# Attention inside a mixture-of-experts layer: PE's projection matmuls and VectorE's work in another order over the eight steps of a unit, and the squares of the roots on GpSimd

## What is computed

```python
q = x @ Wq.T                      # x is layer-normalised
k, v = context @ Wk.T, context @ Wv.T
q, k = rmsnorm(q), rmsnorm(k)     # t * rsqrt(mean(t*t) + 1e-6), per head
attn = softmax(q @ k.T * 16 ** -0.5)
x = x + attn @ v
x = x + moe(layernorm(x))         # 7 experts, 2 per token, and a shared one
```

## Time and profile before

| | us |
|---|---|
| median of 3 runs | 1032.24 |
| lowest, highest | 1028.94, 1035.53 |
| the profiled execution's own time | 1035.61 |
| its span | 1033.8 |
| PE busy, share of the span | 968.9, 94% |
| VectorE busy | 704.0, 68% |
| ScalarE busy | 515.9, 50% |
| GpSimd busy | 145.5, 14% |

### The profile page before, as it was taken

How to read it: one execution, slowest core, us unless ns; L and a number is a source line. 1 busy time by engine, 2 the same in 40 slices (tenths; PEclk the granted TensorE clock), 3 DMA queues, 4 the chain that set the end, 5 groups by cost and what they waited for, 6 DMA issues and landing times.

```text
span 1033.8 us, 18059 instructions
## 1 busy us (share of the span) xinstructions
PE 968.9 (94%) x6730; PEld 701.5 (68%) x6731; DVE 704.0 (68%) x1463; ACT 515.9 (50%) x649; POOL 145.5 (14%) x167
## 2 busy tenths in 40 slices
PE   4899999989999899987799999999999999999995
PEld 3534443345434453332699999999999998999995
DVE  5778767867687756771678776675766767767553
ACT  4578668856787568875334221332423343424311
POOL 1000000000000000000100000233333332433331
PEclk9999999999999999999699999999999999999998
DMA  9100100001000010210342114354363545554533
GB/s 342 66 1 2 41 1 1 4 18 62 1 2 21 11 52 1 83 41 1 103 165 63 62 62 175 74 174 77 74 173 61 183 71 163 148 128 95 152 60 41
DMA packets 28984, 78.93 MB, mean 76 GB/s; under 512 B 7040, under 2 KB 7040, under 8 KB 24832
## 3 DMA queue, kind: packets, MB, share of 16 engines
q1 hardware_dynamic: 18400, 52.31, 14.1%
q0 software_dynamic: 10528, 25.87, 12.5%
HBM read 57.64 MB, written 20.52 MB: 76 GB/s over the span
## 4 chain that ended last, share of the span: by engine, by line
PE 48%; DVE 2%; issue 1%; DVEq 0%; POOL 0%; ACT 0%; POOLq 0%
PE u_ps L1185 15%; PE z_ps L1185 15%; PE y_ps L1185 15%; PE xt_ps L1198 2%; PE z_ps L1179 1%; DVE w_sb L1387 1%; PE y_ps L1211 0%; DVE u_lo L1548 0%; DVE stats L1403 0%; DVE x_lo L1397 0%; DVEq L1029 0%; DVE y_sb L1576 0%; POOL out L1129 0%; PE xt_ps L1171 0%; ACT u_hi L1319 0%
## 5 line engine op out<-in xcount | busy, mean ns | idle before, releaser
L612 ACT ACTIVATE probs<-scores 128x2048 f32<-128x2048 f32 x128 | 240.3, 1878 | 80.8 <-PE scores L267 78.0
L1185 PE MATMUL u_ps<-x_hi,w_sb 128*128 128x256 f32 x896 | 168.0, 285 | 5.0 <-issue 3.1
L1185 PE MATMUL z_ps<-u_hi,w_sb 128*128 128x256 f32 x896 | 169.1, 286 | 0.2 <-DVE u_lo L1548 0.2
L1319 ACT ACTIVATE u_hi<-u_ps,b_ug 128x256 fp32r<-128x256 f32 x112 | 47.0, 471 | 203.8 <-PE u_ps L1185 195.6
L1185 PEld LDWEIGHTS u_ps<-x_hi,w_sb 128*128 128x128 f32 x896 | 143.2, 194 | 7.8 <-issue 4.6
L1185 PEld LDWEIGHTS z_ps<-u_hi,w_sb 128*128 128x128 f32 x896 | 142.4, 193 | 0.4 <-DVE u_lo L1548 0.4
L1185 PE MATMUL y_ps<-w_sb,g_hi 128*128 128x512 f32 x448 | 138.7, 391 | 0.4 <-DVE g_lo L1566 0.4
L283 PE MATMUL o_ps<-probs,v_sb 128*17 128x512 f32 x1024 | 137.5, 609 | 1.0 <-ACT probs L612 1.0
L1185 PE MATMUL u_ps<-x_lo,w_sb 128*128 128x256 f32 x448 | 127.7, 285 | 0.0
L1185 PE MATMUL z_ps<-u_lo,w_sb 128*128 128x256 f32 x448 | 127.1, 284 | 0.0
L267 PEld LDWEIGHTS scores<-q_st,k_hi 32*128 32x128 f32 x512 | 25.1, 183 | 123.8 <-ACT probs L612 71.1
(11 more groups left out here) (216 smaller groups left out, 1567.5 us busy)
## 6 DMA issues: line engine op xcount, KB each, us to landing
w_raw<-w_all SPq DMA_DIRECT2D x27, 1024.0 KB, 6.9
ctx_raw<-ctx_t SPq DMA_DIRECT2D x4, 1024.0 KB, 6.4
out<-x_sb SPq DMA_DIRECT2D x16, 256.0 KB
xg<-xn_dram POOLq DMA_DIRECT2D x14, 256.0 KB
x_sb<-x SPq DMA_DIRECT2D x1, 3072.0 KB, 18.0
xn_dram<-xn SPq DMA_DIRECT2D x12, 256.0 KB, 2.0
bd<-b_down SPq DMA_DIRECT2D x9, 256.0 KB
x_sb<-x SPq DMA_DIRECT2D x4, 256.0 KB, 3.8
```

What stands on the lines that cost most here:

```text
L612: nc.scalar.activation(probs[:, t % 2], scores[:], ACT.Exp).then_inc(p_ready, 1)
L1185: ins = nc.tensor.matmul(out_ps, stat[a], mov[b], start=(first and a + b == 0), stop=(last and a == 1), skip_group_check=True)
L1319: last = nc.scalar.activation(u_hi[:, c, :], u_ps[:, b, a, :], ACT.Identity, bias=b_ug[:, par, 0, c:c + 1])
```

## The change

Projections come in portions of any number of matmuls, set by two tables (`first, end` in the list of the 12). `k_turns` can also come behind the weighing of step 6 (`after`), in the units where a batch follows and g is at least 1. The squares of the roots move from ScalarE to a multiplication on GpSimd. In VectorE's order the second stack of q moves from step 4 of the unit before to step 0 of its own unit, `finalize` of half 1 from step 2 to step 1, Newton's step for k from 6 to 5, the context splits from steps 2, 3, 4, 4 to 1, 2, 2, 3, one normalisation for the batch behind from 1 to 2, the statistics from 0, 1, 6, 7 to 2, 2, 3, 6. The second block of new tokens is split whole on VectorE in step 6 (`norm_both`), where ScalarE made its high part in step 7. q's squares on ScalarE move from step 7 to step 6.

```diff
+        K_TURNS = {6: (0, 4), 7: (4, 5), 0: (5, 9), 1: (9, 12)}
+        Q_TURNS = {3: (0, 5), 4: (5, 9), 5: (9, 12)}
...
+            def root2_q(u):
+                pool.wait_ge(rq_ready, u + 1)
+                pool.wait_ge(norm_done, 2 * u if u else 1)
+                nc.gpsimd.tensor_tensor(r2[:], r0[:], r0[:], ALU.mult).then_inc(r2q_ready, 1)
+
+            def root2_k(u):
+                pool.wait_ge(rk_ready, u + 1)
+                if u:
+                    pool.wait_ge(norm_done, 2 * u + 1)
+                nc.gpsimd.tensor_tensor(r2[:], r0[:], r0[:], ALU.mult).then_inc(r2k_ready, 1)
...
             def between(u, s):
                 b, g, more, behind = batch_of(u)
                 ahead = u + 2 < UNITS
+                if s in (0, 1) and u + 1 < UNITS:
+                    k_turns(u + 1, *K_TURNS[s])
...
-                elif s <= 5:
+                elif s in Q_TURNS:
                     if ahead:
-                        q_passes(u + 2, s - 3)
+                        q_turns(u + 2, *Q_TURNS[s])
...
-                elif ahead:
-                    k_chunk(u + 2, 1)
+                    if ahead and not (more and g >= 1):
+                        k_turns(u + 2, *K_TURNS[s])
+                elif s == 7 and ahead:
+                    k_turns(u + 2, *K_TURNS[s])
                     sum_q(u + 2)
+
+            def after(u, s):
+                b, g, more, behind = batch_of(u)
+                if s == 6 and more and g >= 1:
+                    k_turns(u + 2, *K_TURNS[s])
...
-            def root2_q(u):
-                act.wait_ge(rq_ready, u + 1)
-                act.wait_ge(norm_done, 2 * u if u else 1)
-                nc.scalar.activation(r2[:], r0[:], ACT.Square).then_inc(r2q_ready, 1)
...
                 if s == 0:
-                    stat1(0)
-                    if behind and g == 1:
-                        stat(tile_of(b - 1, 2), mv2[:, 2, :])
                     if more and g == 2:
                         norm_both(b + 1, 2)
+                    if u:
+                        stack_q(u, 1)
...
+                    if more and g == 2:
+                        context_split(b + 1, 0)
                     if nxt:
                         first_root_q(u + 1)
-                elif s == 2:
-                    if more and g == 2:
-                        context_split(b + 1, 0)
                     if u:
                         finalize(u - 1, 1)
+                elif s == 2:
                     if nxt:
                         sums_k(u + 1)
+                    if behind and g == 2:
+                        norm2(b - 1, 1)
+                    if more and g == 2:
+                        context_split(b + 1, 1)
+                        context_split(b + 1, 2)
...
                     if nxt:
                         first_root_k(u + 1)
-                        stack_q(u + 1, 1)
+                        stack_q(u + 1, 0)
...
-                    if more and g == 2:
-                        context_split(b + 1, 2)
-                        context_split(b + 1, 3)
...
+                    if nxt:
+                        newton_k(u + 1)
                     finalize(u, 0)
...
                     if more and g == 1:
                         norm_low(b + 1, 0)
+                        norm_both(b + 1, 1)
```

More of the change, by code:

```diff
@@ L292, in three, with q_turns @@
                 return ins
-            def q_passes(u, part):
+            TURNS = [(c, a, b) for c in range(DC) for a, b in ((0, 0), (0, 1), (1, 0))]
+            def q_turns(u, first, end):
                 g = u % GROUPS
-                if part == 0:
+                if first == 0:
                     begin("b", B_AT, ("q", u), b_free)
@@ L299, in q_passes @@
                     pe.wait_ge(xt_split, (u // GROUPS + 1) * BT)
-                turns = [(c, a, b) for c in range(DC) for a, b in ((0, 0), (0, 1), (1, 0))]
-                for c, a, b in turns[4 * part:4 * part + 4]:
+                for c, a, b in TURNS[first:end]:
                     last = nc.tensor.matmul(bank_b[:], (wq_hi, wq_lo)[a][:, g, c, :], (xt_hi, xt_lo)[b][:, c, :],
@@ L313, in k_chunk @@
                     pe.wait_ge(ctx_split, (u // GROUPS + 1) * MT)
-                last = three(bank_a[:], (wk_hi[:, g, c, :], wk_lo[:, g, c, :]), (ctx_hi[:, c, :], ctx_lo[:, c, :]),
-                             c == 0, c == DC - 1)
-                if c == DC - 1:
+                for c, a, b in TURNS[first:end]:
+                    last = nc.tensor.matmul(bank_a[:], (wk_hi, wk_lo)[a][:, g, c, :], (ctx_hi, ctx_lo)[b][:, c, :],
+                                            start=(c == 0 and a + b == 0), stop=(c == DC - 1 and a == 1),
+                                            skip_group_check=True)
+                if end == len(TURNS):
                     last.then_inc(a_ready, 1)
@@ L442, in _ @@
             v_all(scores[:, 3, :], 0, 3).then_inc(first_v, 1)
-            for part in range(3):
-                q_passes(1, part)
-            k_chunk(1, 0)
-            k_chunk(1, 1)
+            q_turns(1, 0, 12)
+            k_turns(1, 0, 5)
             sum_q(1)
@@ L849, in step @@
                         norm(b + 1, 0)
+                    stat1(0)
+                    stat1(1)
+                    if behind and g == 1:
+                        stat(tile_of(b - 1, 2), mv2[:, 2, :])
                 elif s == 3:
@@ L904, in step @@
                     if more and g == 1:
+                        norm(b + 1, 2)
+                    if behind and g == 2:
+                        norm2(b - 1, 2)
+                else:
+                    if behind and g == 2:
+                        gates_out(b - 1, 0)
+                    if u + 2 < UNITS:
+                        sums_q(u + 2)
+                    if more and g == 1:
                         norm(b + 1, 3)
+                    if nxt:
+                        stack_k(u + 1, 1)
                     if behind and g == 1:
```

111 lines of the change are left out of this document (38 added, 73 removed).

## The result

| | before | after |
|---|---|---|
| median of 20 runs each, us | 1031.59 | 1028.50 |
| lowest, highest | 1028.87, 1035.63 | 1023.33, 1029.82 |
| ratio after/before, 95% interval | | 0.9966 [0.9957, 0.9976] |
| the profiled execution's own time, its span | 1035.61, 1033.8 | 1028.14, 1026.4 |

The change makes the kernel 3.1 to 3.5 us faster, which is within 1%. The forecast of 1024.6 gave it twice that, and the range 1018.0 to 1031.0 held the result. The two profiled executions differ by 7.5 us, almost exactly the 7.6 of the forecast: the first thing to explain is why the medians differ by less than half of it.

What follows compares the result with a forecast made beforehand. PE was taken to carry the attention loop, with waits for VectorE and the exponential's chain. Gains of 3.8, 2.3, 0.2, 3.7, 10.6 less 0.6, 0.2, 7.0, 1.4, 3.8 gave 7.6 us: 1032.2 to 1024.6, range 1018.0 to 1031.0.

Steps and rivals of the forecast that it cites:

- I take the differences over as they are: Gains counted in one profiled execution of 1035.6 us were subtracted unchanged from the median of 1032.24, 3.4 lower.
- the term of 2.3 us for the squares: Step 2 without ScalarE's square returns to 2.72 us, 0.33 gained in each of seven units: 2.3 us.
- the portions' term: Moving projection matmuls between steps gains 0.27 us in each of 14 units, 3.8 us, less 0.6 in seven.
- GpSimd's squares: Each takes 0.51 to 2.7 us, 1.4 taken; hidden in the loop, costing 0.2 us before it.
- Rival B: GpSimd holds VectorE up 0.5 us in units 1, 2, 6, 10, and the clock falls in all four: 1030.4; chance 0.15.
- New tokens: Steps 6 and 7 of units 1, 5, 9: the 1.2 us wait before the q sums goes, 3.7 us gained.
- I find the bank free before PE asks: In units 1, 5, 9, the earlier VectorE split and k behind the weighing leave PE no wait for the bank.
- Units 6 and 10: VectorE's new order removes three waits in steps 4 and 5 and the fallen clock: 5.3 us each, 10.6 together.
- rival D: Waits in steps 4 and 5 of units 6 and 10 stay; half the 10.6 us remains: 1029.9; chance 0.10.
- The new wait: The stack moved to step 0 delays the k sums in units 1, 2, 6, 10: -7.0 us, bounds 0 and -12.
- The clock: Waits of 2.05 us make it fall in units 6 and 10, 1.9 us each: -3.8; units 1, 2 left out.
- rival A: The clock stays up behind the new waits, so the gain is 11.4 us: 1020.8; chance 0.25.

Runs made afterwards that it cites:

- second profile of before: The kernel before, unchanged, run and profiled again: 1030.82 us, ratio 0.9995; the loop of this profile takes 438.7 us against 442.4 in the first.
- e_squares: The kernel before with only the squares of the k and q roots moved from ScalarE to GpSimd: 1032.48 us, ratio 1.0025.
- e_kpool: The kernel before with only k's root squares moved to GpSimd, q's staying on ScalarE: 1032.65 us, ratio 1.0008.
- e_tokens: The kernel before with the new portions, the second new-token block split on VectorE in step 6, and k behind the weighing in units 1, 5, 9: 1026.87 us.
- e_best: Kernel before plus portions, new-token part, respread context splits, one normalisation later, k's root squares on GpSimd, k's Newton step in 5, q's squares in 6: 1018.39 us.
- e_undo_gp: The kernel after with root squares back on ScalarE, k's Newton step back in step 6 and q's squares in step 7: 1027.08 us, ratio 0.996.
- e_stack: The kernel after with q's second stack back in step 4 of the unit before, for units 1, 2, 6 and 10 only: 1025.2 us, ratio 0.994.
- the second session: Both kernels run again unchanged: before 1030.82 us, ratio 0.9995; after 1028.48 us, ratio 0.997.
- e_vfirst: The kernel after with PE taking v ahead of the k sums in step 2 of units 2, 6 and 10, VectorE's order matched: 1028.44 us, ratio 0.9968.

## Why the prediction was right in kind and twice too large

**The step that failed** is "I take the differences over as they are". The sum was made against an execution of 1035.6 us and taken off a median that was lower, as if both had lost the same to the clock. The second profile of before shows 3.7 us of low clock, in units 10, 14 and 15, that come and go. My sum booked the fall of unit 10 as something the change would remove. In the profiled pair it was right to 0.1 us (7.5 against 7.6), and that was luck: units 14 and 15 gave 3.1 us there (24.73 to 23.16, 21.45 to 19.95), where the sum has 0.2, and 2.2 of them are low clock that the second profile of before does not have. Against that profile the loop gains 4.1. Of the 3.5 us to the forecast, 1.6 are the fall of unit 10, which was not there to be removed, and 2.0 are unit 2, which lost 3.5 us where the sum takes 1.5; the rest cancels.

**Portions and squares**: forecast 0.27 and 0.33 for a plain unit, 0.60 together; measured 0.58 together (23.08, forecast 23.1). But alone the portions give 0.50 and the squares 0.30. The two are not a sum: with the square still on ScalarE, step 2 takes 3.05 and the fifth matmul of step 3 hides behind it (2.79); without it, step 2 takes 2.72 and step 3 3.01. So the term of 2.3 us for the squares, sized right against the old portions, is worth 0.08 to 0.10 in each of seven units beside the new ones, 0.6 to 0.7 us, and the portions' term was undersized by about as much.

**GpSimd's squares**: 1.04 us, in the range of 0.51 to 2.7 and near the 1.4 taken. They are not free in the loop. Rival B's first half, that GpSimd holds VectorE up, is shown by e_squares and e_kpool with 0.44 and 0.66 us, where it took 0.5, and in the kernel after by unit 1. The Trainium skill (GPSIMD Engine Reference, Elementwise side-by-side cycle accounting) gave an estimate of 1.1, and these rows agree.

**New tokens**: the wait before the q sums went and unit 5 came to 24.27 where 24.0 was forecast, but not for the reason I gave. e_tokens has all that I named and gains 0.15; without GpSimd, the earlier Newton step and the earlier squares of q the unit stays at 25.51. "I find the bank free before PE asks" held. What I left out was the next in line: VectorE's copy of the q sums, for which ScalarE's logarithm holds up the exponential, and k's stack. The three moves that bring them in time were made together in e_best and undone together in e_undo_gp; that it is the Newton step, which leaves VectorE's queue ahead of both, is read from the rows and was not tested alone.

**Units 6 and 10**: the waits in steps 4 and 5 went, so rival D fell: step 4 from 4.25 to 3.21, step 5 from 9.60 (with a fall in it, 8.00 without) to 5.72; step 6 gave back 0.44. Units 6 and 10 came to 36.32 and 36.41, just above the 35 to 36 named. One reading behind the term was wrong: step 4 did not lose a stack of q. The first stack moved from step 3 into it when the second left, so by its end VectorE is rid of one stack all the same.

**The new wait** before the k sums came in just the four units forecast. Its size was 1.74, 2.03, 2.25 and 2.28 us for units 1, 2, 6 and 10, against 1.3, 1.55, 2.05 and 2.05: 8.3 instead of 7.0. e_stack shows that the moved stack causes it. In unit 1, 0.65 of it is GpSimd's block: e_undo_gp waits 1.09 there.

**The clock**: I took falls in units 6 and 10 and left unit 2 out, since its wait would be 1.55. It fell there too, in both profiles of after. Unit 2 came to 33.23 where 31 was forecast. Beside e_undo_gp, which has the wait and not the fall, the step with the fall, step 2, is 1.3, 1.5 and 1.6 us longer in units 2, 6 and 10, where 1.9 was booked for each of the last two (the whole units differ by 1.5, 0.95 and 1.0, since other steps differ too). So rival A, a clock that stays up, did not come, and of B's four units three fell and unit 1, with 1.74, did not. One of the 20 runs of after took 1023.33 us with a mean clock of 0.983, where the profiled one has 0.979. I read it as a run with fewer of these falls, as I do 1024.93 us with 0.983 among the twelve of the second session, but neither has a profile of its own.

**What stays open** is why the clock fell behind waits of 2.03 to 2.28 us in both profiles of after and behind none of 2.25 to 2.27 in e_undo_gp. It is hardly chance between the two: their mean clocks are 0.978 to 0.980 in 30 of 32 runs of after and 0.981 to 0.986 in all nine of e_undo_gp. Yet a fall is not fixed by the kernel either: behind a wait of 1.8 us in unit 10, step 5, before fell in one profile and not in the other. The two kernels differ in the squares, in the Newton step, and so in when PE runs what (step 0 of unit 2 is 3.58 us in after, 2.75 in e_undo_gp); these were not taken apart.

## What to carry to other kernels

Profile the kernel before twice, and add up a change only against the pattern of low clock that both profiles share; the single execution here, 0.4% above the median, carried 3.7 us of low clock that came and went without any edit. Where an in-order queue is full in one stretch, moving a piece of it earlier or later moves the wait (e_stack, e_vfirst, e_tokens each did), and what helps is to spread the pieces that nothing needs soon, here the context splits. An operation given to an idle engine is not free if it holds up, as GpSimd's squares did VectorE's rows, the engine that others wait for, and it should be placed where that engine has slack.
